# The last part of a two-layer AdaLN kernel: the next pair's output products, residual and first norm inside the present pair

## The reference, cut to what matters

```
# layer 0
h  = norm(x) * (1 + scale_a) + shift_a
o  = recurrent_attention(h)                 # scan over chunks of 16 tokens
x  = x + gate_a * ((o * (h @ Wg.T)) @ Wo.T) # output products "wo", first residual
h  = norm(x) * (1 + scale_b) + shift_b      # norm 1 of the last part
x  = x + gate_b * (gelu(h @ U1 @ V1 + b1) @ U2 @ V2 + b2)
# layer 1
h  = norm(x) * (1 + scale_c) + shift_c      # norm 2
x  = x + gate_c * (local_attention(h) @ Wp) # window of 64 keys and 4 global ones
h  = norm(x) * (1 + scale_d) + shift_d      # norm 3
x  = x + gate_d * (sigmoid(xr @ W_r) * (relu(xk @ W_k)**2 @ W_v))   # xr, xk mix h with h of the token before
```

## Time and profile before

| | before |
|---|---|
| median of 3 runs | 2673.7 us (2673.67 to 2675.98) |
| the profiled execution | 2678.21 us, span 2676.4 us |
| mean granted TensorE clock | 0.949 |
| PE / PEld busy | 2314.9 us (86%) / 1456.5 us (54%) |
| DVE / ACT / POOL busy | 1603.7 (60%) / 1575.9 (59%) / 1095.1 us (41%) |

### The profile page before, as it was taken

One profiled execution on the slowest core, in us unless ns is written; L12 is line 12 of the kernel. 1 busy time (PEld: TensorE's weight loads), 2 busy tenths in 40 slices (PEclk: granted clock), 3 DMA queues, 4 the chain that ended last, 5 costly groups with the idle time before them and its releaser, 6 DMA issues.

```text
span 2676.4 us, 90848 instructions
## 1 busy us (share of the span) xinstructions
PE 2314.9 (86%) x33549; PEld 1456.5 (54%) x33549; DVE 1603.7 (60%) x3880; ACT 1575.9 (59%) x4079; POOL 1095.1 (41%) x1208
## 2 busy tenths in 40 slices
PE   5999994788887878886699999999999999999998
PEld 4545542455555555554367475564655656647566
DVE  2888885666666666665265474663744736537365
ACT  1878885666656666665264483563835737447365
POOL 0122221566666666667423344133332343323423
PEclk8999997888988998998899999999999999999999
DMA  5455556523322323311421302202132022220220
GB/s 173 138 156 159 156 170 143 101 51 80 78 65 67 77 64 79 74 29 33 126 48 49 88 23 78 48 26 88 30 94 47 26 70 48 76 66 26 70 48 17
DMA packets 404872, 206.35 MB, mean 77 GB/s; under 512 B 273938, under 2 KB 389778, under 8 KB 404388
## 3 DMA queue, kind: packets, MB, share of 16 engines
q1 hardware_dynamic: 404420, 200.37, 28.4%
HBM read 106.38 MB, written 71.38 MB: 66 GB/s over the span
## 4 chain that ended last, share of the span: by engine, by line
issue 33%; PE 33%; POOL 15%; DVE 9%; ACT 5%; DMA 2%; SPq 1%; POOLq 0%; DVEq 0%; ACTq 0%
POOL arena L1654 7%; PE psum L747 6%; PE psum L835 3%; DVE arena L1719 3%; PE psum L830 3%; PE psum L1013 3%; PE psum L1021 3%; ACT arena L1261 2%; PE psum L823 2%; PE psum L843 2%; PE psum L814 2%; POOL arena L1666 1%; PE psum L973 1%; PE psum L1004 1%; DVE arena L1728 1%
## 5 line engine op out<-in xcount | busy, mean ns | idle before, releaser
L1654 POOL TENSOR_TENSOR arena<-arena 128x400 f32<-128x400 f32 x256 | 218.2, 853 | 492.1 <-DVE arena L2029 492.1
L1261 ACT ACTIVATE arena<-psum,scan_sb 64x128 f32<-64x128 f32 x1152 | 308.1, 361 | 148.6 <-PE psum L904 82.7
L1445 ACT ACTIVATE arena<-psum,arena 128x100 f32<-128x100 f32 x1024 | 269.8, 366 | 6.6 <-DVE arena L2021 6.6
L1719 DVE SCALAR_TENSOR_TENSOR arena<-psum,taps_sb,arena 128x511 f32<-128x511 f32 (+2 forms) x288 | 213.7, 747 | 60.6 <-ACT arena L1170 53.8
L747 PE MATMUL psum<-arena,w_in_sb 128*128 128x512 f32 x512 | 229.9, 598 | 0.9 <-issue 0.9
L1477 POOL TENSOR_TENSOR arena<-arena 128x512 f32<-128x512 f32 x64 | 79.5, 1272 | 360.9 <-ACT arena L1196 360.9
L1501 POOL TENSOR_TENSOR arena<-arena 128x512 f32<-128x512 f32 x132 | 139.6, 1057 | 209.3 <-ACT arena L1289 209.2
L1786 DVE TENSOR_TENSOR arena<-psum,scan_sb 64x512 f32<-64x512 f32 x290 | 186.1, 674 | 36.0 <-PE psum L922 28.8
L966 PE MATMUL psum<-mask_sb,identb 128*128 128x400 bf16 x960 | 202.5, 347 | 0.0
L1437 ACT ACTIVATE arena<-psum 100x512 f32<-100x512 f32 x256 | 156.1, 610 | 49.3 <-PE psum L1087 43.0
L2021 DVE TENSOR_REDUCE arena<-psum 128x4 f32<-128x400 f32 x256 | 146.3, 573 | 62.5 <-PE psum L1074 50.8
(11 more groups left out here) (212 smaller groups left out, 4926.4 us busy)
## 6 DMA issues: line engine op xcount, KB each, us to landing
arena<-arena SPq DMA_DIRECT2D x144, 128.0 KB
arena<-x SPq DMA_DIRECT2D x32, 512.0 KB, 4.1
arena<-gates_d SPq DMA_DIRECT2D x116, 128.0 KB, 4.5
arena<-o_d SPq DMA_DIRECT2D x18, 512.0 KB, 7.3
arena<-gate_d SPq DMA_DIRECT2D x18, 512.0 KB, 8.4
v_rows_d<-arena SPq DMA_DIRECT2D x64, 136.0 KB
k_rows_d<-arena SPq DMA_DIRECT2D x64, 136.0 KB
arena<-k_rows_d SPq DMA_DIRECT2D x128, 68.0 KB, 2.0
```

Of the source, the lines that this page charges most:

```text
L1261: ins = act.activation(dst.rearrange("p (t x a) -> p t x a", x=PP, a=INNER)[upper, :, x], src.rearrange("p (t a) -> p t a", a=INNER)[upper ...
L1445: act.activation(c_soft[s][:, f % 2, u], sc, ACT.Exp, bias=c_max[s][:, u:u + 1]).then_inc(c_act.mark(f"exp{s}{f}u{u}"), 1)
L1654: pool.tensor_tensor(soft, soft, c_rec[s].unsqueeze(2).broadcast_to([P, 4, KEYS]), ALU.mult).then_inc(c_pool.mark(f"prob{s}{f}"), 1)
L1719: ins = dve.scalar_tensor_tensor(out=a_acc[:, t, j:TOK], in0=bank[2 + t][:, 0:TOK - j], scalar=taps_sb[:, t % KT, col:col + 1], in1=a_acc[ ...
```

## The change

The head of a turn is taken out of the loop and made a set of steps of its own (`n_pe`, `n_dve`, `n_act`, `n_pool`) that run one pair ahead. The output products of the next pair stand on TensorE behind `v2`, in place of the 22 fillers of norm 2; the residual and the statistics of the next pair on DVE behind the present pair's norm 2; the normalised rows behind the mixing of norm 3; the transposes ahead of each slot's `vv`; the modulation at the end of ACT's turn. For that the rows have a place of their own, `n_x`, with their statistics. The fillers of the head (10, 6, 6) and those before `vt` (8, 6) are gone, but for `norm2` in the last pair. `q` now waits for the next pair's residual, since it writes the banks of `wo`. Each engine's loop has 7 turns, and the last pair is written out behind it (`pair(LAST, False)`); the first pair's head stands ahead of it. The arena grows from 36816 to 38176 elements a partition. `o_d`, `gate_d` and `gates_d` lose their two extra entries and the DMAs that filled them.

```
-            for past in (o_d, gate_d):
-                sp.dma_start(past[BATCH:BATCH + AHEAD]..., x[0:AHEAD]...).then_inc(ahead_filled, 16)
-            sp.dma_start(gates_d[BATCH:BATCH + AHEAD], gates_row[0:AHEAD]).then_inc(gates_stored, 16)
...
# SP, one pair (before: rows and wp gates first, outputs behind the wv gates)
+            def pair(i, before, ahead, ahead2):
+                if before:
+                    store_rows(i - 1)
+                    load_gates_ffn(i)
+                    load_gates(i, "wv", c_wv, 3)
+                if ahead:
+                    for s in SLOTS:
+                        sp.wait_ge(c_dve.sem, c_dve.at(i, f"x2{s}1"))
+                        load_rows(i + 1, s)
+                    sp.wait_ge(n_pool.sem, n_pool.at(i + 1, "oz1"))
+                frame_values(i)
+                if ahead2:
+                    next_weights(i + 2)
+                if ahead:
+                    for s in SLOTS:
+                        sp.wait_ge(c_pe.sem, c_pe.at(i, f"pv{s}{FRAMES - 1}"))
+                    if ahead2:
+                        for s in SLOTS:
+                            load_outputs(s, i * 2 + s + 2 * len(SLOTS))
+                    sp.wait_ge(c_pe.sem, c_pe.at(i, "wp11"))
+                    load_gates(i + 1, "wp", c_wp, 2)
...
# TensorE
+            def next_out(n):
+                for s in SLOTS:
+                    pe.wait_ge(n_pool.sem, n_pool.at(n, f"wo{s}"))
+                    pe.wait_ge(n_pool.sem, n_pool.at(n, f"oz{s}"))
+                    rows_out(s, n_pe, "wo", lambda k, t: c_oz[s][:, k, tok(t)], lambda k: c_wo[s][:, k], (3, 0))
+            def next_turn(n, s):
+                pe.wait_ge(n_dve.sem, n_dve.at(n, f"xh{s}3"))
+                turn_rows(s, n_pe, "t", (2, 3))
...
+                for s in SLOTS:
+                    pe.wait_ge(n_act.sem, n_act.at(i, f"h{s}1"))
+                        mm = pe.matmul(B(s, 3)[half(s)], u1_sb[:, k], c_h[s][:, k, 1:TOK + 1], ...)
+                for s in SLOTS:
+                    pe.wait_ge(c_dve.sem, c_dve.before(i, f"rv{s}1"))
...
-                        stay_warm("norm2", B(1, 0))
-                    turn_c(s, 2, (3, 0))
-                    stay_warm(f"vt{s}", B(1, 0) if s == 0 else B(0, 3))
+                if ahead:
+                    next_out(i + 1)
+                else:
+                    stay_warm("norm2", B(1, 0))
+                for s in SLOTS:
+                    turn_c(s, 2, (1, 2))
+                for s in SLOTS:
                     pe.wait_ge(c_act.sem, c_act.at(i, f"h2{s}{KT - 1}"))
...
+                        if which == "q" and ahead:
+                            pe.wait_ge(n_dve.sem, n_dve.at(i + 1, f"x{s}1"))
...
                 for s in SLOTS:
+                    if ahead:
+                        pe.wait_ge(c_act.sem, c_act.at(i, f"kk{s}1"))
+                        next_turn(i + 1, s)
                     pe.wait_ge(c_pool.sem, c_pool.at(i, f"kk{s}1"))
...
# DVE
                 norm(2, "v2", (1, 2))
+                if ahead:
+                    next_rows(i + 1)      # per slot: 2 residual adds, 4 statistics, 4 aggregates
... (copies of vt)
+                if ahead:
+                    next_scale(i + 1)     # 2 reciprocals
... (q, k, attention, norm 3, xr and xk)
+                if ahead:
+                    for s in SLOTS:
+                        dve.wait_ge(c_pe.sem, c_pe.at(i, f"turn3{s}{KT - 1}"))
+                        next_normal(i + 1, s)   # 1 small copy, 4 normalised tiles
...
# ACT, behind the last kk
+                if ahead:
+                    for s in SLOTS:
+                        act.wait_ge(c_dve.sem, c_dve.at(i, f"xk{s}{KT - 1}"))
+                        if s == 1:
+                            act.wait_ge(c_pool.sem, c_pool.at(i, "d1"))
+                        next_modulate(i + 1, s)
```

More of the change, by code:

```diff
@@ L34 @@
 LAYERS = 2
-AHEAD = 2
-ARENA = 36816
+ARENA = 38176
 ALU = mybir.AluOpType
@@ L1367, in _, with next_std, next_modulate, pair @@
             last_cols(2)
-            with act.Fori(0, BATCH // 2) as i:
-                B = lambda s, j: bank[4 * s + j]
+            B = lambda s, j: bank[4 * s + j]
+            def next_std(n):
+                for s in SLOTS:
+                    act.wait_ge(n_dve.sem, n_dve.at(n, f"ag{s}{TT - 1}"))
+                    act.activation(n_std[s], n_mv[s][:, :, 1], ACT.Sqrt, bias=parity[:, 6:7]).then_inc(n_act.mark(f"std{s}"), 1)
+            def next_modulate(n, s):
+                for k in range(KT):
+                    act.wait_ge(n_pe.sem, n_pe.at(n, f"t{s}{k}"))
+                    act.activation(c_h[s][:, k, 1:TOK + 1], B(s, 2 + k)[:], ACT.Identity, bias=n_modb[s][:, k:k + 1],
+                                   scale=n_modb[s][:, KT + k:KT + k + 1]).then_inc(n_act.mark(f"h{s}{k}"), 1)
+            next_std(0)
+            for s in SLOTS:
+                next_modulate(0, s)
+            def pair(i, ahead):
                 def std(stage, s):
```

267 lines of the change are left out of this document (144 added, 123 removed).

## The result

| | before | after |
|---|---|---|
| median, us (runs) | 2674.8 (4) | 2568.5 (4) |
| lowest to highest, us | 2673.7 to 2684.5 | 2558.9 to 2580.9 |
| ratio, 95% interval | | 0.960 (0.955 to 0.965) |
| profiled execution, its span, us | 2678.2, 2676.4 | 2580.9, 2579.1 |
| part three, us (its first memset to the end of the span) | 1401.5 | 1293.6 |

The change saves 106 us, 4.0%. The forecast was 2566 us with a range of 2555 to 2582. The profiled execution of the changed kernel is the slowest of its four, and it is late ahead of the changed code: part three begins at 1285.5 us in it and at 1274.9 us in the kernel before. In the profiled executions of the kernels further down it began between 1258.5 and 1281.1 us.

The account below looks back on a forecast made before the run. TensorE, busy 86%, was held by a late serial chain at each turn's head. Heads 108.5 less norm 2's 2.8 plus 2 and 0.4 for first and last pair save 108.1 us: 2566 us, range 2555 to 2582.

Parts of the forecast that it names:

- two of the signs that were to speak for its rivals: Clock under 1.00 from `wo` to `q` or `kk` to `v1`; a POOL or ACT row releasing `wo`, `u1` or `v1`.
- The head: Last `kk` to first `v1`: 12.6 us against 28.2; gain at the seven heads 147.66 - 39.2 = 108.5 us.
- The margins: Slack between `vv` and `v1`: ACT's loop end 1.7 us before the first `u1` copy; DVE's `rv` the thinnest.
- The rival of a new wait: Late gated outputs, ACT's loop end or late x rows cost 2 to 3 us a turn: 2580 to 2587 us; 11 in 100.
- Norm 2: `wo` replaces the fillers, 7 us of products for 0.4 us a turn, 2.8 us in seven turns.
- The clock rival: Clock falls in norm 2 around the 16 transposes and 2.4 us idle: 8.4 to 12 us, 2574 to 2578; 22 in 100.
- The price of DVE's added work: Next pair's adds and statistics behind norm 2, 6.5 us with gaps, done before either `q` needs them: no cost.
- the forecast's own range: 2558 to 2573 us around 2566, given 62 in 100.
- First and last pair: First pair's head gains 2 us, bounds 3 lost and 5 won; last pair's norm 2 saves 0.4 us.
- The frames: Rival: framed values miss the first value product, since x rows delay the `vt` copies; slower than before; 2 in 100.
- the hidden head: Rival: the block of Gelu is bound elsewhere and the head's time returns there; 2650 us up to no change; 1 in 100.
- The sum: Whole kernel: 108.5 - 2.8 + 2 + 0.4 = 108.1 us saved.

Follow-up runs that it names:

- half of the change: Changed kernel with the next pair's normalised rows, transposes and modulation back at the turn's head; `wo`, residual and statistics stay ahead: 2615.8 us, ratio 0.974.
- the copies first: Changed kernel with DVE's two copies of `vt` ahead of the next pair's residual and statistics instead of behind them: 2593.3 us, ratio 0.966.
- the second profile of the kernel: The changed kernel run and profiled once more without any edit: 2565.8 us, ratio 0.957 to the kernel before.
- the run with the spare Gelu: Changed kernel plus a one-column Gelu, its result unread, on ACT at each turn's head ahead of the copies of `u1`: 2563.4 us, ratio 0.957.
- filled with twelve products: Changed kernel with 12 filler products between norm 2's transposes: 2558.6 us, ratio 0.954; with five more fillers at attention's start: 2553.6 us, ratio 0.953.
- `wo` was split: Changed kernel with the last quarter of `wo` between norm 2's transposes: 2558.7 us, again 2557.9; with five fillers at attention's start: 2543.6 us, ratio 0.949.
- the run with both edits: Changed kernel with the last quarter of `wo` between norm 2's transposes and a one-column unread Gelu at ACT's turn head: 2558.9 us, ratio 0.953.

## Why the prediction was right

**Number and mechanism.** The median fell into the stated range, and the moved work bought what it was to buy. But two of the signs that were to speak for its rivals came too: the clock fell in norm 2, and TensorE waits for an ACT row ahead of `v1`. Errors of both signs met in the sum.

**The head.** Forecast 12.6 us from the last `kk` to `v1`; measured 11.5 to 12.1 in the seven turns. It was right as a sum of two terms that were wrong. The two `u1` were put at 3.72 us, twice the 1.86 of the earlier trace rows. They take 2.05 us together: the slots' products, 64 output partitions each, run beside each other once nothing stands between them. Against that stood 0.63 us of "issue" on TensorE where the loop turns, and 0.56 us for ACT's copies, which the sum had at nothing. In the kernel before `wo` followed `vv` without such a gap, and no run shows why. DVE's rows for it took 2.11 us a slot instead of the 1.38 of the sum, since GpSimd was at work beside them, and still stood 4.1 us ahead of the transposes. The experiment with half of the change gives the chain's price: put back, it costs 6.5 us a turn.

**The margins.** ACT's at its loop end, given as 1.7 us, held: it stood idle for 1.40 us ahead of its first copy and waited for TensorE. What TensorE waits for, 0.56 us a turn, is the copy itself. The forecast had slot 0's copy beside slot 1's `u1`; since both `u1` end together, nothing covers it. POOL's gated outputs ended 1.4 us ahead of `wo`. The rival of a new wait was thus right by its sign at one place, for a reason that it did not have and at a fifth of its price (0.6 instead of 2 to 3 us), and the overlap of `u1` paid for it.

**Norm 2.** Forecast +0.4 us a turn; measured +0.16 us (20.06 against 19.90) where the clock holds. The wait was given as 2.4 us and is 2.25. The price of DVE's added work, put at nothing, held: `q` starts with `vt`'s end. The run with the copies first shows that this rested on the order on DVE.

**The clock rival.** It was given 22 in 100, and its mechanism came true: in four of seven pairs, at 1.6 us each, within its 1.2 to 1.7, or 6.4 us; in the second profile of the kernel in six, 9.9 us. It did not carry the total out of the forecast's own range because the heads gave 5.2 us more than summed; that was luck. In the second profile the two further falls in norm 2 were matched by two fewer at the start of attention.

Over all profiles of kernels with `wo` ahead, the seven turns of each show how far the wait decides. Where it was left at 2.25 us (up to 2.71 in the run with the spare Gelu) the clock fell in 27 of 35 turns, 4 to 7 in each of five profiles. Where it was filled with twelve products it fell in none of 14, and where `wo` was split and 0.97 us were left, in none of 28. So the stretch as it stood is a condition of the fall. It isn't enough by itself: of pairs with the same wait and the same 16 transposes some fell and some did not, and what decides between them stays open. In both profiles of the changed kernel all pairs but the first fell at exactly one of the two places, norm 2 or attention's start, and the first at both; with the copies first, where `q` waits too, most fell at both.

The prediction weighed the Trainium skill's rule (TensorE: Matmul & The Clock Gate, the section on PE-mode transpose) that transposes don't count as work for the clock. The traces speak against the near certainty that the prediction read out of it: four of the fourteen norm 2 stretches of the two profiles stayed at 1.00. Whether the 2.25 us of idle or the whole stretch without other products is what counts, no run separates, since the fillers and the quarter of `wo` fill the one and break up the other. The wait at attention's start, 1.23 us, has score products and no transposes before it, and the clock fell there as well.

**First and last pair.** For the first pair's head forecast +2 us, measured -0.5, inside its bounds of 3 lost and 5 won; for the last pair forecast +0.4, measured +0.8. Counted from the part's first memset, `wo` started at 13.0 us instead of 16.6 and the x rows landed at 20.3 instead of 22.4, so both gains came; the two slots' statistics in series used them up, and the first transposes stand at 28.4 as before (28.3). The whole head ran at the lower level for longer than before (10.1 us for `wo` against 8.8, and 1.97 us for each group of transposes against 1.10). DVE's second group of normalised rows took 3.41 us, with POOL's product beside it:

```profile
1313.83 3.41 DVE L2035 TENSOR_SCALAR arena<-arena 128x256 f32<-128x256 f32 x4
...
1313.92 2.52 POOL L1700 TENSOR_TENSOR arena<-arena 128x1024 f32<-128x1024 f32 x1 [10.34 <-DVE arena L2032]
```

**The frames and the hidden head.** Both rivals are out. The first value products wait for no DMA: the last frames are issued 8.8 us ahead of them. The run with the copies first moved the frames by 1.3 us only and so adds little. The head was not hidden: `kk` to `v1` fell by 113.7 us in seven turns, and the block behind it did not grow (134.2 against 135.2 us).

**The sum.** 107.9 us of part three against 108.1. The median is 2.5 us over the forecast. That this is so close is in part luck, since errors met: 5.2 us more at the heads than summed (113.7 against 108.5), 1.5 more in the stages costed at nothing and 0.4 in the last pair, 4.7 less in norm 2 and 2.5 less in the first pair.

## What to carry to other kernels

Moving a serial chain's links one by one into waits that already exist is worth the chain's time plus that of the clock falls which its waits cause; what is moved has to stand, on each engine, so that the work which frees the next products' banks comes first. A clock fall saved at one wait can turn up at the next: look at all idle stretches of a turn before you price one, and close them together. Fillers are not waste to be dropped by their busy time: taking 58 a turn out of the kernel before cost 3.9 us a turn. And before a lost gain is put down to the clock, read the granted clock of the stretch: in the run with both edits it was 1.00, and the loss came from GpSimd's memsets beside DVE's rows.

## What was not expected of the hardware

- Two groups of four products with 64 output partitions each, in different column halves, took 2.05 us together and 1.86 us alone.
- The end of a loop's turn shows as "issue" on each engine: 2.4 to 2.9 us on DVE, 1.9 to 2.5 on ACT, up to 1.1 on TensorE (0.6 in most turns of the changed kernel). Whether it counts depends on what the others do: in the kernel before, DVE's 2.5 us passed while TensorE made `wo`.
- ACT loads a table at the head of a turn before a mere copy, 1.28 us, and another for the Gelu right behind the copies. A Gelu placed first left one of the two.
- DVE's group of four TENSOR_SCALAR of 128x256 takes 1.38 us alone, 2.11 us beside POOL's 128x512 products at the end of a turn, 3.41 us beside its 128x1024 product and up to 2.81 us beside its memsets in norm 2. One tile of the four takes all of it: 2.44 us instead of 0.41 beside the 128x1024 product of 2.52 us. The Trainium skill (Advanced Engine Details and Errata, VectorE Performance Modes) has the rule that DVE's second SBUF port is shared with GpSimd, so that GpSimd's instructions and DVE's two-port ones block each other. The traces agree: in part three of all 13 profiles every such tile over 0.42 us had a POOL instruction beside it, and no tile without one was slow. Which port an instruction used, no trace shows. The residual adds of the same turns, which read PSUM, took 1.25 to 1.29 us for two throughout.
- Parts one and two, the same code in all kernels here but for some DMAs, ended between 1258.5 and 1285.5 us from one profiled execution to the next, more than most of the edits above are worth.
